# Row blocks of a causal-attention layer turned by VectorE and DMA in place of TensorE, and the first block handled by two tiles

## What is computed

```python
x = x + attn(layernorm(x))       # causal attention, one head: q=(y@Wq+bq)/16, k=y@Wk+bk, v=y@Wv+bv,
                                 # softmax over the keys up to the own row, then @Wo + bo
x = x + ffn(layernorm(x))        # r = sigmoid(xr@W_r), k = relu(xk@W_k)**2, out = r * (k@W_v)
# xr, xk mix a row with the row before it: mu*x + (1-mu)*x_prev
```

## Time and profile before

| | |
|---|---|
| median of 3 runs | 365.44 us (364.97 to 365.71) |
| profiled execution | 365.21 us, of which span of the core 363.2 us |
| PE busy | 353.2 us, 97% of the span, granted clock 1.00 |
| DVE, ACT, POOL busy | 254.8, 239.2, 209.0 us |

### The profile page before, as it was taken

The page is one execution under the profiler, slowest core; times in us unless marked ns, Lnnn a source line. Parts: engine busy times, 40 slices in busy tenths (PEclk is TensorE's granted clock), DMA queues, the critical chain, the costliest instruction groups (busy, mean ns, idle before and its releaser), DMA issues.

```text
span 363.2 us, 6783 instructions
## 1 busy us (share of the span) xinstructions
PE 353.2 (97%) x2466; PEld 324.5 (89%) x2466; DVE 254.8 (70%) x569; ACT 239.2 (66%) x467; POOL 209.0 (58%) x246
## 2 busy tenths in 40 slices
PE   8999999999999999999999999999999999999995
PEld 6788888989899888899998989999999999989885
DVE  4597888698946786855568876786857558673645
ACT  2355543987659547597565679587368877789572
POOL 4013330468777743579644357678155768699781
PEclk9999999999999999999999999999999999999999
DMA  7600000000012003003000000030000000000001
GB/s 214 220 2 1 2 0 3 0 3 1 2 38 79 1 0 117 1 2 90 28 3 0 2 0 3 29 88 1 3 29 31 0 3 2 30 31 0 31 29 58
DMA packets 11905, 10.64 MB, mean 29 GB/s; under 512 B 1889, under 2 KB 11874, under 8 KB 11874
## 3 DMA queue, kind: packets, MB, share of 16 engines
q1 hardware_dynamic: 10512, 10.23, 8.8%
q10 hardware_dynamic: 1362, 0.01, 0.2%
HBM read 6.04 MB, written 4.19 MB: 28 GB/s over the span
## 4 chain that ended last, share of the span: by engine, by line
PE 76%; DVE 8%; POOL 6%; ACT 5%; issue 3%; DMA 1%; SPq 0%; ACTq 0%; DVEq 0%
PE W L794 16%; PE W L797 16%; PE W L798 15%; PE O L961 7%; PE O L963 7%; PE O L962 7%; PE W L830 3%; POOL kT_hi L364 3%; DVE mix L710 2%; DVE h_row L696 1%; POOL mix_lo L369 1%; DMA h_row<-in_L_attn_Wq_dram 1%; DVE st L675 1%; ACT mix L471 1%; ACT st L416 1%
## 5 line engine op out<-in xcount | busy, mean ns | idle before, releaser
L364 POOL TENSOR_TENSOR p_lo<-st,p_hi 128x512 fp32r<-128x512 f32 (+1 forms) x71 | 80.9, 1157 | 38.8 <-ACT p_hi L416 37.7
L663 DVE TENSOR_TENSOR peak<-peak,W 128x512 f32<-128x512 f32 (+3 forms) x70 | 42.2, 603 | 47.9 <-ACT st L416 47.7
L416 ACT ACTIVATE st<-W 128x512 f32<-128x512 f32 (+1 forms) x79 | 42.5, 538 | 42.3 <-PE W L798 42.2
L961 PE MATMUL O<-v_hi,p_hi 128*128 128x258 f32 x241 | 69.1, 287 | 0.2 <-DVE x_in L685 0.2
L963 PE MATMUL O<-v_hi,p_lo 128*128 128x258 f32 x241 | 68.0, 282 | 0.0
L962 PE MATMUL O<-v_lo,p_hi 128*128 128x256 f32 x241 | 67.7, 281 | 0.0
L797 PE MATMUL W<-xT_lo,kT_hi 128*128 128x512 f32 (+2 forms) x188 | 65.9, 350 | 0.0
L794 PE MATMUL W<-xT_hi,kT_hi 128*128 128x512 f32 (+2 forms) x188 | 64.4, 343 | 0.8 <-DVE kT_lo L573 0.8
L798 PE MATMUL W<-xT_hi,kT_lo 128*128 128x512 f32 (+2 forms) x188 | 63.2, 336 | 0.0
L452 ACT ACTIVATE st<-st 128x512 f32<-128x512 f32 (+1 forms) x79 | 44.8, 567 | 8.7 <-DVE st L675 8.6
L416 ACT ACTIVATE p_hi<-st 128x512 fp32r<-128x512 f32 (+1 forms) x71 | 40.4, 569 | 15.3 <-PE O L963 13.4
(11 more groups left out here) (138 smaller groups left out, 824.3 us busy)
## 6 DMA issues: line engine op xcount, KB each, us to landing
out_dram<-gate SPq DMA_DIRECT2D x15, 256.0 KB, 2.1
x_in<-in_L_attn_y_all_dram SPq DMA_DIRECT2D x7, 512.0 KB, 4.5
x_in<-in_L_attn_y_all_dram SPq DMA_DIRECT2D x2, 256.0 KB, 4.8
h_row<-in_L_attn_Wk_dram SPq DMA_DIRECT2D x1, 256.0 KB, 3.1
h_row<-in_L_attn_Wq_dram SPq DMA_DIRECT2D x1, 256.0 KB, 4.3
st<-in_L_attn_Wv_dram SPq DMA_DIRECT2D x1, 256.0 KB, 5.3
st<-in_L_attn_Wo_dram SPq DMA_DIRECT2D x1, 256.0 KB, 5.5
mix<-in_L_ffn_W_k_dram SPq DMA_DIRECT2D x1, 256.0 KB, 6.6
```

The source lines that it names most:

```text
L364: g.tensor_tensor(lo[:, r], score_tile(u), hi[:, r].bitcast(f32), ALU.subtract).then_inc(p_split, 1)
L416: a.activation(dst, src, ACT.Copy, **kw).then_inc(done, 1)
L663: v.tensor_tensor(peak[:, J % 2, r], peak[:, J % 2, r], scores, ALU.max).then_inc(maxed, 1)
L961: mm(o[:, 0:VW], hi[:, r], v_hi[:, j + b, :], start=j + b == 0, stop=False)
```

## The change

Three things. First, for blocks 2 to 7 (`XF = 2`) TensorE no longer transposes xhat. VectorE turns xhat in place in 32x32 blocks, two tiles an instruction (512 elements a partition), SP then moves the 32-row squares between partitions with 16 DMAs a block (16 = 4 by 4 squares; each moves 32 partitions by 8 runs of 128 bytes) into `xT_lo`, ScalarE writes `xT_hi` from there (SBUF, not PSUM), and GpSimd, not VectorE, subtracts it in place to leave the low part. The `W` banks have no xT use for these blocks. In the diff `xT_low` is GpSimd's, the two pieces after it are ScalarE's, and the last, which follows the apply of a tile, is VectorE's. Second, in the start block 0 is handled by two tiles: the fold of `wkq` runs by d and is copied by halves, xT of tiles 0 and 1 goes ahead of tiles 2 and 3, kT is made in column halves; the fillers are fewer. Third, all slot tables are new, and SP's work is put in slot order with them.

```diff
+    XF = 2
+    SIDE = 32
+    SQ = P // SIDE
+    MOVES = 16 * SQ * SQ
...
-    APPLY_AT = {1: (1, 1), 2: (4, 5), 3: (17, 17), 4: (32, 33), 5: (40, 40), 6: (44, 44), 7: (61, 61)}
-    XT_AT = {1: (2, 2), 2: (7, 9), 3: (23, 23), 4: (33, 34), 5: (43, 43), 6: (47, 50), 7: (61, 61)}
-    KT_AT = {1: (5, 5), 2: (12, 17), 3: (25, 31), 4: (36, 36), 5: (44, 45), 6: (51, 53), 7: (66, 66)}
+    XM_AT = {2: (8,), 3: (18,), 4: (29,), 5: (40,), 6: (45,), 7: (62,)}
+    STATS_AT = {1: (-3, -2), 2: (1, 2), 3: (4, 5), 4: (26, 26), 5: (36, 37), 6: (42, 42), 7: (54, 55)}
+    APPLY_AT = {1: (1, 1), 2: (3, 4), 3: (13, 16), 4: (27, 27), 5: (39, 39), 6: (43, 43), 7: (56, 56)}
+    XT_AT = {1: (2, 2), 2: (9, 9), 3: (20, 22), 4: (31, 34), 5: (42, 42), 6: (45, 45), 7: (62, 62)}
+    KT_AT = {1: (4, 5), 2: (11, 12), 3: (26, 29), 4: (38, 38), 5: (45, 45), 6: (58, 58), 7: (63, 65)}
...
-    IDLE = (6, 1, 5, 6, 1)
+    IDLE = (6, 1, 3, 0, 0)
...
+            def move(src, dst, done):
+
+                rows = src.rearrange("p k t (b i) -> p (k t) b i", i=SIDE)
+                channels = dst.rearrange("p k (t a i) -> p (k t) a i", a=SQ, i=SIDE)
+                for a in range(SQ):
+                    for b in range(SQ):
+                        sp.dma_start(channels[b * SIDE:(b + 1) * SIDE, :, a, :], rows[a * SIDE:(a + 1) * SIDE, :, b, :]).then_inc(done, 16)
+
+            def move_x(G):
+                sp.wait_ge(x_turned, 2 * (G - XF + 1))
+                if G >= NT:
+                    sp.wait_ge(s_ready, FIRST[last_group(G - NT) + 1])
+                    sp.wait_ge(v_ready, 2 * (G - NT + 1))
+                move(xhat, xT_lo[:, G % NT].bitcast(f32), x_moved)
...
+            def xT_low(G, h):
+                pool.wait_ge(xT_high, KC * G + h + 1)
+                g.tensor_tensor(xT_lo[:, G % NT, h], xT_lo[:, G % NT, h].bitcast(f32), xT_hi[:, G % NT, h].bitcast(f32), ALU.subtract)\
+                    .then_inc(x_split, 1)
...
+                elif h == 0:
+
+                    sc.wait_ge(x_moved, MOVES * (G - XF + 1))
+                high(xT_hi[:, G % NT, h], bank_of("xT", G, h)[:] if G < XF else xT_lo[:, G % NT, h].bitcast(f32), xT_high)
...
             for h in range(KC):
-                xT_part(0, h)
+                sc.wait_ge(fold_ready, 3 + h)
+                high(wkq_hi[:, h, :], folded[h][:, 0:C], fold_moved, scale=SCALE)
+            for i in range(2):
+                sc.wait_ge(xT_ready, i + 1)
+                high(xT_hi[:, 0, :, i * 2 * P:(i + 1) * 2 * P], pairs(bank_of("xT", 0, i)), xT_high)
...
+                elif G >= XF and t % 2 == 1:
+
+                    dve.wait_ge(xhat_done, TG * G + t + 1)
+                    v.memset(xhat[:, 0, t - 1:t + 1, 0:1], 1.0).then_inc(xhat_ready, 1)
+                    dve.wait_ge(xhat_ready, XF + 1 + 2 * (G - XF) + t // 2 + 1)
+                    rows = xhat[:, :, t - 1:t + 1, :].rearrange("p k t c -> p k (t c)")
+                    v.transpose(rows, rows).then_inc(x_turned, 1)
```

More of the change, by code:

```diff
@@ L131, in stages @@
+    FF_AT = [(25, 25), (33, 34), (40, 41), (52, 52), (64, 67), (141, 155), (177, 177), (547,), (551,), (1111,)]
+    END = 1112
+    FT_AT = [(-3,), (3,), (5,)]
+    IDLE = (6, 1, 3, 0, 0)
     def stages(s):
         found = []
-        for name, table in (("mt", MT_AT), ("mix", MIX_AT), ("apply", APPLY_AT),
+        for name, table in (("mt", MT_AT), ("xm", XM_AT), ("mix", MIX_AT), ("apply", APPLY_AT),
                             ("stats", STATS_AT), ("hT", HT_AT), ("kk", KK_AT), ("rr", RR_AT), ("ff", FF_AT),
@@ L246, in attention_channel_mix_block @@
         early = (bank_o + bank_w[:NO - 1:-1])[:4]
+        folded = (bank_b, early[0])
         def o_of(G, p):
@@ L311, in _, with store @@
                 load(G)
[L312 to L324, removed]
+            def move(src, dst, done):
[10 more added lines that the diff above has]
+                move(xhat, xT_lo[:, G % NT].bitcast(f32), x_moved)
+            def store(J, i):
+                G, t0, n = PARTS[J]
+                if J in SINGLE:
+                    sp.wait_ge(last_out_ready, SINGLE.index(J) + 1)
+                    sp.dma_start(out_t[:, G * TG + t0, :], gate[:, t0, :]).then_inc(stored, 16)
+                    return
+                t = t0 + 2 * i
+                sp.wait_ge(out_ready, unit(J, i) + 1)
+                if i == 1 and G + NX < NG:
+                    load(G + NX)
+                sp.dma_start(out_t[:, G * TG + t:G * TG + t + 2, :], gate[:, t:t + 2, :]).then_inc(stored, 16)
+            for s in SLOTS:
+                for stage, n, i in STAGES[s]:
+                    if stage == "ff":
+                        store(n, i)
+                    elif stage == "xm":
+                        move_x(n)
             sp.wait_ge(stored, 16 * (2 * NG - 1 + len(SINGLE)))
@@ L405, in _ @@
                         rsqrt1(n)
+                    elif stage == "xT" and n >= XF:
+                        xT_low(n, i)
                     elif stage == "kk" and n < LAST:
@@ L634, in _ @@
                 ln1_apply(0, t)
[L635 to L637 removed]
             for h in range(KC):
[L639 to L640 removed]
+                dve.wait_ge(fold_moved, h + 1)
+                v.scalar_tensor_tensor(wkq_lo[:, h, :], folded[h][:, 0:C], SCALE, wkq_hi[:, h, :].bitcast(f32), ALU.mult, ALU.subtract)                    .then_inc(fold_split, 1)
+            for i in range(2):
+                c = slice(i * 2 * P, (i + 1) * 2 * P)
+                dve.wait_ge(xT_high, i + 1)
+                low(xT_lo[:, 0, :, c], bank_of("xT", 0, i)[:].rearrange("p (k c) -> p k c", k=KC), xT_hi[:, 0, :, c], xT_split)
+            taken(early[2], wvT, 5, 1)
             for h in range(KC):
                 kT_part(0, h)
[L643 removed]
+            dve.wait_ge(fold_moved, 3)
             low(wvo_lo[:], early[0][:].rearrange("p (k c) -> p k c", k=KC), wvo_hi[:], fold_split)
@@ L826, in free, with turned, queries_ready, first_xT @@
                     pe.wait_ge({"xT": xT_split, "kT": kT_split, "v": v_split, "hT": mu_done, "kk": k_relu}[stage], 2 * g + i + 1)
-            def transposes(bank, src, h, tiles):
+            def turned(bank, src, tiles):
                 for t in tiles:
-                    last = nc.tensor.transpose(bank[:, t * P:(t + 1) * P], src[:, t, h * P:(h + 1) * P], ident[:])
+                    last = nc.tensor.transpose(bank[:, t * P:(t + 1) * P], src[:, t, :], ident[:])
                 return last
+            def queries_ready(G):
+                if G < XF:
+                    pe.wait_ge(xT_split, KC * (G + 1))
+                else:
+                    pe.wait_ge(x_split, KC * (G - XF + 1))
+            def first_xT(i):
+                pe.wait_ge(xhat_ready, i + 1)
+                for h in range(KC):
+                    for t in range(2):
+                        last = nc.tensor.transpose(bank_of("xT", 0, i)[:, (2 * h + t) * P:(2 * h + t + 1) * P], xhat[:, h, 2 * i + t, :], ident[:])
+                last.then_inc(xT_ready, 1)
             def xT(G, h):
                 free("xT", G, h)
-                pe.wait_ge(xhat_ready, G + 1)
-                transposes(bank_of("xT", G, h), xhat, h, range(TG)).then_inc(xT_ready, 1)
+                pe.wait_ge(xhat_ready, G + 2)
+                turned(bank_of("xT", G, h), xhat[:, h], range(TG)).then_inc(xT_ready, 1)
             def kT(G, h):
                 free("kT", G, h)
-                pe.wait_ge(xT_split, KC * (G + 1))
-                if G == 0:
-                    pe.wait_ge(fold_split, 1)
+                queries_ready(G)
                 project(bank_of("kT", G, h)[:], wkq_hi, wkq_lo, slice(h * P, (h + 1) * P),
@@ L998, in _ @@
             pe.wait_ge(taken_ready, 1)
-            pe.wait_ge(q_taken, 1)
-            for h in range(KC):
-                for d in range(KC):
-                    last = mm(bank_b[:, h * C:(h + 1) * C], wkT[:, d, h * P:(h + 1) * P], wqT[:, d, :], start=d == 0, stop=d == KC - 1)
-            last.then_inc(fold_ready, 1)
+            for d in range(KC):
+                pe.wait_ge(q_taken, d + 1)
+                for h in range(KC):
+                    last = mm(folded[h][:, 0:C], wkT[:, d, h * P:(h + 1) * P], wqT[:, d, :], start=d == 0, stop=d == KC - 1)
+                    if d == KC - 1:
+                        last.then_inc(fold_ready, 1)
```

102 lines of the change are left out of this document (47 added, 55 removed).

## The result

The changed kernel takes 372.61 us, the median of 4 runs (371.29 to 372.92), and the kernel before, run beside it, 365.56 us (364.97 to 365.71). The ratio is 1.0189, with a 95% interval of 1.0162 to 1.0216: it is slower by 7 us, where 5.8 us less were forecast, and lies outside the range. The profiled execution took 372.61 us, with a span of 370.8 us.

A forecast was written before the change was run, and what follows sets the result against it. The prediction took TensorE, busy for 97% of the span, as the bound. It summed -5.2 (transposes) - 1.1 (start) + 0.5 (VectorE) = -5.8 us, from 365.44 to 359.6 us, with a range of 356.8 to 364.4 us.

The forecast's parts named there:

- Part 2: VectorE: 12 turns replace 12 low parts, total unchanged (-2.3 to +2.6 us); waits in the full early stretch, +0.5 us.
- Part 3: ScalarE reads SBUF instead of PSUM and GpSimd gains 12 subtractions of 1.31 us, 15.7 us: hidden, 0.
- Part 6: New slot tables move work, not its amount: 0, between -2 and +2 us.
- Part 1: TensorE: 48 transposes of blocks 2 to 7 go, at 0.109 us each: -5.2 us.
- Part 4: SP's moves for blocks 2 to 7: about 9 us each, 14.5 at most, all hidden: 0.
- my limits of 14 and more: Moves of blocks 2 to 7 cost nothing up to about 14, 14, 15.5, 21, 16 and 20 us.
- The 4.2 us that I added for the `W` banks: If ScalarE waits for a move, TensorE goes on until the third later bank use, about 3 x 1.4 us.
- Rival 1: Slow moves of 128-byte pieces, decisive from about 16.3 us each: 380 us at 20, 421 at 27; chance 0.17.
- Part 5: Start, block 0 by two tiles: kT ends about 1.1 us earlier, -1.1 us (bounds 0.4 and 1.6).
- Rival 3: VectorE or GpSimd bounds crowded stretches; two or three waits of 1.5 to 2.6 us: 362 to 366 us; chance 0.10.

The follow-up runs named there:

- experiment 17: experiment 2 with two extra turns on VectorE for block 3, the second undoing the first, nothing moved: 364.82 us, ratio 0.9982.
- 18: experiment 2 with extra pairs of turns on VectorE for blocks 2 to 7 (12 instructions), nothing moved: 373.26 us, ratio 1.0221.
- experiment 9: experiment 2 with block 3 alone turned and moved, at its old slots, GpSimd making the remainders: 371.69 us, ratio 1.0170.
- experiment 13: experiment 9 with VectorE, not GpSimd, subtracting for the low part of block 3: 366.35 us, ratio 1.0025.
- experiment 4: The changed kernel with the subtraction that makes xT_lo on VectorE instead of GpSimd: 372.50 us, ratio 1.0200.
- kernel 1: The changed kernel with its new tables and start, but TensorE transposing all eight blocks and no moves: 379.94 us, ratio 1.0401.
- experiment 3: The changed kernel with one of the 16 transfers of a block: 370.34 us, ratio 1.0138.
- experiment 2: The kernel before, old slot tables and TensorE's transposes, with only the new start by two tiles: 363.35 us, ratio 0.9946.
- 14: experiment 2 with blocks 3 and 5 turned and moved in the old order, remainders on VectorE: 367.03 us, ratio 1.0044.
- 12: The changed kernel with xT of block 6 in slot 47, not 45, and its kT in slots 55 and 56, not 58: 367.38 us, ratio 1.0057.
- 16: kernel 1 with xT of block 6 in slot 47 and its kT in slots 55 and 56: 375.50 us, ratio 1.0267.
- 7: kernel 1 with the old tables of statistics, apply, xT, kT and fT, the new ones for all else: 395.64 us, ratio 1.0818.
- experiment 8: The changed kernel with 8 and 10 filler matmuls in TensorE's two long waits (slot 46, ahead of step 59): 370.12 us, ratio 1.0121.
- 11: The changed kernel with only kT of block 6 moved, to slots 55 and 56 from 58: 368.65 us, ratio 1.0091.

## Why the prediction was wrong

**The step that failed** is the costing of parts 2, 3 and 6 by busy share: VectorE's total "stays as it is" and "off the path", GpSimd's 15.7 us "Hidden, 0", and the tables "move work, not its amount", "0, between -2 and +2". I took a share of 70% or 63% to mean that an engine has room. Its place in line decides. TensorE has three `W` banks; each product needs one that ScalarE or VectorE has read, and these take their work in order. What is put in front of a maximum or a low part can go to TensorE's wait in full: in the old order 1.42 us of turns cost 1.5 (experiment 17) and 8.5 us cost 9.9 (18), and two remainders behind four others on GpSimd, which was 58% busy before, cost 5.3 us for one block (9 against 13). It need not: 3 us more on VectorE cost nothing in experiment 4.

**Part 1, the transposes: right, with a term left out.** Work at normal spacing fell by 7.2 us, of which the transposes are the 5.2 forecast. In the new order, turning in place of transposing gains 7.3 us (1 against the changed kernel) with what the transfers cost already paid. The 5.2 us of transposes don't cover that. What I left out is that xT also takes `W` banks: in kernel 1 that makes the wait of 4.78 us and the lower clock after it. Against this the changed kernel has its own waits, at 201 and 248 us, so the 7.3 is a difference of a few large waits and no price for each transpose.

**Part 2, the turn:** 0.711 us for 0.679 forecast, right in size. VectorE's total didn't stay: it rose by 6.3 us, beyond my 2.6, and 4.7 of that are `xhat` and `h_row`, whose instructions got longer (`xhat` from a mean of 409 ns to 493, `h_row` from 607 to 671). Near 20 to 30 us TensorE is busy for 8.58 us where it was 9.56, 1.0 us of waiting for 0.5. That is luck: the three waits there start TensorE again at 23.94, 25.10 and 27.08 us, and the first turn begins at 28.8. I looked only there, the one stretch in which VectorE was full over 10 us; most of the losses came later, at 200 and 245 us among others, where VectorE is full over 5 us (4.79 and 4.78).

**Part 3:** a remainder takes 1.29 us, as forecast. Its cover exists only in the new order, where on VectorE it would cost the same (experiment 4); in the old order its place was the largest single loss.

**Part 4, the move: the piece right, the issue wrong.** 12.1 ns a piece for 13.5. The term for 16 issues was mis-sized: 10.4 to 11.8 us, not 6.2 to 7.4. A move takes 12.3 to 13.7 us and not 9, still within my limits of 14 and more; yet it costs 0.8 us, or up to 2.3 with the clock (experiment 3), where I had 0. ScalarE waited for it three times, for blocks 2, 3 and 6. It was free for the copies 11.3, 11.2 and 10.5 us after the second turn had ended, and I had 10, 10 and 12: this part of the account was right, and the move was too long for it. The 4.2 us that I added for the `W` banks hid most of it. The move of block 2 lies whole on the chain that ended last, from its first issue at 32.28 us to ScalarE's copy at 44.82. Rival 1, the slow move, was wrong: it gave 380 us and more. The Trainium skill, DMA: Bandwidth & Descriptors, section Why small descriptors are slow (HBM only), exempts transfers within SBUF from the penalty for small pieces. The trace agrees: 12.1 ns is under the straight line between 4 bytes and 1 KB. The read-modify-write below 512 bytes that the same page's section Specifications states doesn't show in that number, which is far from the 97 ns of my rival 1.

**Part 5, the start: right.** `kT` started where forecast and ended 1.0 us earlier, for 1.1. The 1.9 us of experiment 2 hold another 1.0 us from near 129 us, which no part of the sum had, and which kernels 9, 13, 14 and 18, with the same start, don't keep.

**Part 6, the tables: the largest term, put at 0.** With TensorE's transposes the new order costs 16.6 us. Two places are known: xT of block 6 at slot 45 and its kT at slot 58, together 5.2 us with turned rows and 4.4 with TensorE's transposes (12, 16). The remaining 12 us are not located, and the one division of the tables that was tried (7) doesn't divide them. The clock is a part of the loss that no step had: 2.5 us in the changed kernel (8).

**Rival 3** had the mechanism, VectorE or GpSimd the bound in crowded stretches, with the right kind of waits (1.5 to 2.5 us) and too small a price: 362 to 366 us and a chance of 0.10. As a sum of two or three waits it could not end slower than before by more than 1 us; the order alone makes more.

**Why it is slower, in short.** In the old order turned rows lose what they take from TensorE. For block 3 alone (13, matched with 2 start by start) the turns cost 1.2 us and the missing transposes give 0.9; the score step that waits for the remainders costs 0.5, and two waits for VectorE behind it 0.7 near 89 us and 0.6 near 98. The last 0.9 of the 3.0 us is the wait near 131 us that the kernel before has too and kernel 2 escaped by luck, so the block itself costs about 2. In the new order turned rows gain, but that order costs more than they bring. Why the order costs the rest is open, and so is whether a third order would make them pay; no kernel here with turned and moved rows beat 366.35 us.

## What to carry over

The busy share of an engine doesn't say whether more work on it is free: look, slot by slot, at what stands behind the new instruction in its queue and which bank or operand TensorE takes next; with few banks in flight it can cost its whole length, as in 17, or nothing, as in 4. An order tuned for one set of operations is a part of the cost: run the new order with the old operations, and the new operations in the old order, before either is called free. Here the piece worth keeping was the smallest, the first block by two tiles: 363.35 us against 372.61 and 365.56, of which 1.0 us is the start's own.

## What was unexpected of the hardware

VectorE and GpSimd slow each other when VectorE reads two operands from SBUF: 0.65 us became 1.20 and 1.27 us became 1.51 (experiment 13), and the mix instructions at 241.58 us took 1.32 us, with a mean of 0.915 in that kernel. `h_row`, which reads one array and two columns, is hit as well: the least of its 32 instructions took 402 ns in the changed kernel, the longest 1403. The Trainium skill, SBUF — State Buffer, states in its section SBUF: two separate sides that a VectorE instruction with two SBUF inputs and a GpSimd one that reads SBUF share a pair of ports, which the first to come holds for its whole instruction. The trace agrees that they collide; in experiment 13 both got longer. Before, near 126 us, the `h_row` that started 0.01 us after GpSimd's instruction of 1.31 us took 1.45 us in place of 0.41, so it ended 0.15 us after that instruction did.

The granted clock of TensorE fell to 0.73 and 0.66 over 5 us after waits of 2.0 and 2.5 us in the changed kernel, and to 0.73 and 0.59 around the wait of 5.36 us in experiment 9. With matmuls in the waits it stayed at 1.00 (experiment 8). The length of a wait alone doesn't decide: kernels 3 and 11 have the same wait of 2.0 us for `kT_lo` and kernel 18 one of 2.7 us, and their clock stays at 1.00 behind it.

Issues of transfers in a row cost 0.65 to 0.74 us each on SP's queue, with 256 pieces of 128 bytes in each, against 0.39 for a single store; the median issue took 0.61 us, the longest 1.63. The loads at the start stand in a row too and took 0.45 to 0.48 us each for 256 KB, so standing in a row doesn't explain all of it. What does was not tried.
